# A state-space scan in one instruction over two PSUM banks instead of two instructions over one bank each

## What is computed

```python
deltaA = jnp.exp(jnp.einsum('bld,dn->bldn', delta, A))
deltaBu = jnp.einsum('bld,bln,bld->bldn', delta, B, u)
...
def step(h, inputs):
    dA_t, dBu_t, C_t = inputs
    h = h * dA_t + dBu_t
    y = jnp.einsum('bdn,bn->bd', h, C_t)
    return (h, y)
```

## Time and profile before

| | |
|---|---|
| median of 3 runs | 934.71 us (930.47 to 934.96) |
| profiled execution, its own time | 937.12 us |
| span of its trace, first to last instruction | 935.3 us |
| PE busy | 845.0 us (90%) |
| DVE busy | 633.1 us (68%) |
| ACT busy | 364.7 us (39%) |
| POOL busy | 349.3 us (37%) |
| mean granted TensorE clock | 0.955 of full speed |

### The profile page before, as it was taken

How to read it: one execution, slowest core, us unless ns; L and a number is a source line. 1 busy time by engine, 2 the same in 40 slices (tenths; PEclk the granted TensorE clock), 3 DMA queues, 4 the chain that set the end, 5 groups by cost and what they waited for, 6 DMA issues and landing times. The chain is left out here.

```text
span 935.3 us, 12349 instructions
## 1 busy us (share of the span) xinstructions
PE 845.0 (90%) x4548; PEld 632.7 (68%) x4548; DVE 633.1 (68%) x1218; ACT 364.7 (39%) x739; POOL 349.3 (37%) x337
## 2 busy tenths in 40 slices
PE   6898986788998999998999999997796999999996
PEld 5676754667536778876537878875134787738885
DVE  5342478998946278998944479996999877526222
ACT  5120345763273254443272354444384322261110
POOL 5300426851303047861312139840457521202221
PEclk9898997999998999999999999998789799999999
DMA  6202041023020244440020154321200123313542
GB/s 230 107 6 82 1 160 43 1 80 106 2 113 1 82 159 136 136 134 15 2 112 1 34 159 136 113 93 46 91 1 1 35 68 109 129 35 116 165 140 74
DMA packets 26927, 76.10 MB, mean 81 GB/s; under 512 B 3436, under 2 KB 5420, under 8 KB 26228
## 3 DMA queue, kind: packets, MB, share of 16 engines
q1 hardware_dynamic: 26612, 75.26, 24.2%
q10 hardware_dynamic: 256, 0.07, 0.0%
HBM read 74.13 MB, written 1.11 MB: 80 GB/s over the span
## 5 line engine op out<-in xcount | busy, mean ns | idle before, releaser
L915 PE MATMUL B<-late 128*128 128x256 f32 (+2 forms) x1064 | 243.1, 382 | 2.0 <-POOL late L698 1.1
L915 PEld LDWEIGHTS B<-late 128*128 128x128 f32 (+1 forms) x1064 | 199.4, 193 | 32.7 <-POOL late L698 2.0
L1599 DVE TENSOR_TENSOR_SCAN arena<-F,arena 128x512 f32<-128x512 f32 x128 | 149.1, 1206 | 3.3 <-POOL arena L590 2.4
L599 POOL TENSOR_TENSOR arena<-du,arena 128x1024 f32<-128x1024 f32 x60 | 140.9, 2358 | 23.1 <-PE F L915 23.1
L842 ACT ACTIVATE F<-delta,a_neg 128x255 f32<-128x255 f32 x256 | 109.3, 467 | 54.0 <-DVE arena L1599 53.7
L698 POOL TENSOR_TENSOR late<-late 128x512 f32<-128x512 f32 x42 | 53.5, 1275 | 137.4 <-DVE late L1744 101.7
L1609 DVE TENSOR_TENSOR arena<-arena,F 128x1024 f32<-128x1024 f32 x60 | 73.3, 1221 | 8.4 <-PE F L915 2.7
L579 POOL TENSOR_TENSOR rs<-ve,minus_half 128x2 f32<-128x2 f32 (+1 forms) x20 | 15.3, 764 | 165.6 <-DVE ve L1549 75.1
L904 ACT ACTIVATE late<-B 128x512 f32<-128x512 f32 x42 | 24.9, 593 | 93.7 <-PE B L915 93.6
L883 ACT ACTIVATE late<-B 128x512 f32<-128x512 f32 x96 | 51.9, 593 | 18.7 <-PE B L915 17.0
L915 PE MATMUL F<-arena,ident 128*128 128x256 f32 x232 | 57.9, 391 | 0.5 <-DVE arena L1637 0.5
(11 more groups left out here) (357 smaller groups left out, 1466.0 us busy)
## 6 DMA issues: line engine op xcount, KB each, us to landing
late<-in_w_moe SPq DMA_DIRECT2D x112, 384.0 KB, 3.5
room<-in_w_f SPq DMA_DIRECT2D x4, 2544.0 KB, 9.1
arena<-b_out SPq DMA_DIRECT2D x32, 256.0 KB, 5.5
room<-in_w_l SPq DMA_DIRECT2D x4, 768.0 KB, 6.4
w_m<-in_w_m SPq DMA_DIRECT2D x1, 2112.0 KB
room<-in_w_l SPq DMA_DIRECT2D x4, 512.0 KB, 3.7
x_t<-in_x_t SPq DMA_DIRECT2D x4, 256.0 KB, 2.6
x_tok<-in_x_tok SPq DMA_DIRECT2D x4, 256.0 KB, 5.3
```

Source lines behind the costliest of these rows:

```text
L599: g.tensor_tensor(state(n).rearrange("p d (s t) -> p d s t", s=2), du[:, 2 * dp:2 * dp + 2, :].unsqueeze(2).to_broadcast([P, 2, 2, S]), b_ ...
L915: return t_.matmul(dst, lhsT, rhs, start=start, stop=stop, skip_group_check=True)
L1599: v.tensor_tensor_scan(h, F[i][:, :], h, 0.0, ALU.mult, ALU.add)\
```

## The change

The two scans of a step become one instruction that reads the two neighbouring banks F[0] and F[1] as 1024 columns and writes both halves of the state. It waits for the second half of the refill (ACT works in order, so the first is then written too), and in step 0 for POOL's second input. It raises one semaphore step, `scan{n}`, where there were two, and both halves of the next refill wait for that one.

```diff
                 for i in range(2):
                     if n >= 1:
-                        act.wait_ge(*df.at(f"scan{n - 1}_{i}", b))
+                        act.wait_ge(*df.at(f"scan{n - 1}", b))
...
                     n = STEPS.index(ph)
-                    for i in range(2):
-                        h = state(n)[:, i, :]
-                        dve.wait_ge(*af.at(f"dA{n}_{i}", b))
-                        if n == 0:
-                            dve.wait_ge(*df.at("first", b))
-                            dve.wait_ge(*gf.at(f"dbu0_{i}", b))
-                        elif i == 0:
-                            dve.wait_ge(*gf.at(f"dbu{n}", b))
-                        v.tensor_tensor_scan(h, F[i][:, :], h, 0.0, ALU.mult, ALU.add)\
-                            .then_inc(df.step(f"scan{n}_{i}"), 1)
+                    dve.wait_ge(*af.at(f"dA{n}_1", b))
+                    if n == 0:
+                        dve.wait_ge(*df.at("first", b))
+                    dve.wait_ge(*gf.at(f"dbu{n}" if n else "dbu0_1", b))
+                    flat = state(n).rearrange("p i n -> p (i n)")
+                    v.tensor_tensor_scan(flat, banks_f[:, 0:1024], flat, 0.0, ALU.mult, ALU.add)\
+                        .then_inc(df.step(f"scan{n}"), 1)
```

## The result

The changed kernel takes **946.75 us**, the median of 4 runs (944.94 to 948.47). The kernel before took 932.59 beside it (4 runs, 929.38 to 934.96). The ratio is 1.017, with a 95% interval from 1.0141 to 1.0199: 14.2 us slower, where 12.3 were forecast. In the larger samples taken beside the experiments, the kernel before stands at 930.4 (12 runs), 930.3 and 930.1 (23 each). The changed kernel was not timed beside these; set against them, it would cost some 16 us.

What follows compares the result with a forecast made beforehand. DVE was taken to set the pace in stages 0 and 3 and run abreast with PE in 1 and 2. Stage terms 6.4, 2.9, 1.1 and 1.9 sum to 12.3 us; on 934.7, forecast 947.0 us, +1.3%, range 939 to 955.

Steps and rivals of the forecast that it cites:

- The bound: All four stages: DVE sets the pace in 0 and 3, abreast with PE in 1 and 2; PE loses behind DVE.
- rival A: PE has more slack than granted in stages 1 and 2; only 0 and 3 count, 943 or 941 us; chance 0.22.
- The scan itself: Each step's scan on DVE: one wide scan takes 2.27 us instead of 2.33, gaining 0.06 a step, 3.9 at most.
- The rule of one large tile that pays once: All 64 scans: whole fixed part of 0.14 us saved each, 926 us; the faster rival holding this had chance 0.03.
- DVE's busy time: Sign in the changed kernel's profile: DVE's busy time sinks by some 4 us.
- The plain step: Steps with only L1609 between scans: 0.50 us idle less 0.06 for the scan, +0.44, steps 4.01 apart.
- The step with table loads: Stage 0, loads on ACT behind the refill: +1.09 us less cover; steps 3, 5, 9 and 13 together 3.0.
- Tanh behind the refill: Stage 1 experts, L1738 waits for a tanh behind the refill: +0.73 us each at steps 7, 10 and 11.
- Step 0: Stage 0's first scan waits for the whole refill: +0.80 us.
- Stage by stage: Loss summed along the trace's steps: 6.4, 2.9, 1.1 and 1.9 us for stages 0 to 3, 12.3 in all.
- Stage 3: Up to step 9 +1.5 us, steps 13 to 15 +0.7, of which PE's slack takes 0.3: 1.9.
- Rival C: Worse: wide scan takes 2.41 us (7 us more), or the granted clock sinks (3 us); 950 to 957, chance 0.13.

Runs made afterwards that it cites:

- e5: Changed kernel with the wide scan only in sequences 1 and 2, two narrow scans in 0 and 3; 937.62 us, +7.3 against the kernel before.
- e10: Changed kernel with Tanh in place of Silu in sequence 1's feed-forward, so no table loads between stage 0's refills; 944.39 us.
- e12: Kernel before with Tanh in place of Silu in sequence 1's feed-forward, so no table loads there; 929.91 us, ratio 1.0001.
- e11: Changed kernel with four tanh of stage 1 moved on ACT ahead of the refill beside them; 944.67 us.
- e4: Changed kernel with each refill cut from four activations to three from step 1 on; 933.38 us, ratio 1.0036.
- e6: Changed kernel with the wide scan only in sequences 0 and 3, two narrow scans in 1 and 2; 945.26 us, ratio 1.0149.
- e8: Changed kernel, wide scan kept, with every refill after step 0 of a stage left out; 928.26 us, ratio 0.9970.
- e3: Kernel before, two scans kept, but both refill halves wait for the second scan and both scans for the whole refill; 948.76 us, +18.3.
- e1: Kernel before, two scans kept, but both halves of the refill wait for the second scan; 939.21 us, +8.8.

## Why the prediction was right, and where not

**The bound.** DVE was read as setting the pace in stages 0 and 3, and as running abreast with PE in 1 and 2, so that idle time on DVE would be passed on. The stage lengths bear it out in all four; e5 shows it for the middle ones alone, the place where rival A had its chance.

**The scan itself.** Forecast 2.27 us, measured 2.286 (mean of 64, had 1206 ns for 512 columns). The saving is 2.33 - 2.286 = 0.045 us a step instead of 0.06, 2.9 us in all. The rule of one large tile that pays once (the Trainium skill, "VectorE: DVE Perf Modes", "The TRN2 errata") would have given 926 us by the prediction's estimate: the rows disagree, since two neighbouring scans overlap and most of the fixed part was hidden already. DVE's busy time fell by 0.9 us, not by the 4 that were named. The scans gave 2.8; but a scan that starts 0.09 us before the end of L1609 (165.59 against 164.46 + 1.22 = 165.68) counts the common part once. In the trace before, 59 of the 64 steps begin so; in the trace after, 33. The other 26 no longer share some 0.085 us each, 2.2 us together.

**The plain step.** +0.44, 4.01 apart; measured 4.02 with an idle time of 0.41. The idle time ahead of all scans was put at some 20 us and is 15.1. **The step with table loads.** +1.09 at step 5; measured 4.68 - 3.58 = 1.10. e10 and e12 confirm that the cost is there only behind the wide scan. Their sum in stage 0 was put at 3.0 for four steps, plain part included, and came to 3.0 (0.78, 1.10, 0.77 and 0.36); e10 gets 2.5 of it back, since it leaves the plain part where it is.

**Tanh behind the refill.** The timeline of DVE in stage 1, step 7, of the changed kernel:

```profile
383.48 1.22 DVE L1606 TENSOR_TENSOR arena<-arena,F 128x1024 f32<-128x1024 f32 x1
385.62 0.69 DVE L1735 SCALAR_TENSOR_TENSOR late<-late,B 128x512 f32<-128x512 f32 x1 [0.93 <-ACT late L904]
386.41 0.69 DVE L1741 TENSOR_TENSOR late<-late,B 128x512 f32<-128x512 f32 x1
387.02 2.28 DVE L1596 TENSOR_TENSOR_SCAN arena<-F,arena 128x1024 f32<-128x1024 f32 x1
```

From L1606 to the scan 3.54 us, where it was 381.78 - 379.03 = 2.75: +0.79, less 0.045 for the scan, against 0.73 forecast. Here two products lie between the scans, and the scan itself doesn't wait; a wait by what stands behind the refill on ACT costs as much as one by the scan. e11 removes just that.

**Step 0.** Refill to scan:

```profile
142.06 2.29 DVE L1596 TENSOR_TENSOR_SCAN arena<-F,arena 128x1024 f32<-128x1024 f32 x1 [3.60 <-ACT F L842]
```

The refill started at 140.36; 1.70 us, against 143.22 - 142.32 = 0.90: +0.80, as forecast.

**Stage by stage.** Forecast 6.4, 2.9, 1.1, 1.9; measured 5.9 (with step 0), 3.0, 1.0, 4.0. Stage 0 is short of the forecast by 0.5 because of small instructions between steps 0 and 1: the scans of these steps are 10.59 apart where they were 11.33. L1414 took 0.17 instead of 1.98 us there, and L1502 2.17 instead of 1.05. The change does touch them, by way of POOL. The timelines of POOL and DVE, before:

```profile
143.15 9.26 POOL L599 TENSOR_TENSOR arena<-du,arena 128x1024 f32<-128x1024 f32 x4
150.46 1.98 DVE L1414 COPY tr<-v 128x4 f32<-128x4 f32 x1
```

and after:

```profile
140.76 9.26 POOL L599 TENSOR_TENSOR arena<-du,arena 128x1024 f32<-128x1024 f32 x4
150.37 0.17 DVE L1414 COPY tr<-v 128x4 f32<-128x4 f32 x1
```

Before, L1414 starts while POOL is in the last of its four multiplications and ends at 152.44, 0.03 us behind it (143.15 + 9.26 = 152.41). After, the last one has ended (150.02) when L1414 starts. L1502 and L1504 also end 0.03 us behind the end of one of POOL's four, in both. In all 14 traces L1414 takes 1.98 us where it starts before the last of the four has ended, and 0.17 where it starts behind it. So these instructions end by POOL's time, and what the first scan loses ahead of them is in part or whole made up: counted from the start of POOL's four, the scan of step 1 starts at 11.40 before and at 11.89 after, though the first scan starts at 0.07 and 1.30. In e4, e6 and e8 the first scan is wide too, but the refill ahead of it began earlier beside POOL's work: there it starts at 0.86 to 0.87 and the scan of step 1 at 11.37 to 11.39, so that nothing is left of step 0's loss. The prediction had no term for this; without it stage 0 would have cost some 6.7.

**Stage 3 is the step that failed**: "Up to step 9 +1.5, which the 6.66 us wait of PE passes on; steps 13 to 15 add 0.7", 1.9 in all. It was 4.0. ACT's timeline:

```profile
704.44 1.67 ACT L842 ACTIVATE F<-delta,a_neg 128x255 f32<-128x255 f32 x4 [1.36 <-DVE arena L1596]
706.05 2.14 ACT L883 ACTIVATE late<-B 128x512 f32<-128x512 f32 x4
```

PE's timeline, the instructions behind it:

```profile
707.16 0.39 PE L915 MATMUL B<-late,k_t 128*128 128x512 bf16 x1 [2.27 <-ACT late L883]
708.49 0.61 PE L915 MATMUL F<-bcp,pick 128*128 128x256 bf16 x2
708.89 1.91 PE L915 MATMUL F<-arena,ident 128*128 128x256 f32 x4
```

and DVE's:

```profile
706.14 2.29 DVE L1596 TENSOR_TENSOR_SCAN arena<-F,arena 128x1024 f32<-128x1024 f32 x1 [0.41 <-ACT F L842]
...
709.14 1.22 DVE L1606 TENSOR_TENSOR arena<-arena,F 128x1024 f32<-128x1024 f32 x1 [0.71 <-PE F L915]
```

The attention's exps (L883) stand behind the late refill, as the tanh does in stage 1. I had costed that for tanh, and for the exps only by a lump. PE waits 2.27 us for the first of them. The same wait in PE's timeline of the kernel before is 0.79:

```profile
697.21 0.88 PE L915 MATMUL B<-late,k_t 128*128 128x512 bf16 x2 [0.79 <-ACT late L883]
...
698.82 1.03 PE L915 MATMUL F<-arena,ident 128*128 128x256 f32 x4
```

In the changed kernel the granted clock is at its lower level, 1.2 GHz, behind this wait (columns of the earlier trace rows):

```profile
708.00:710.00 2.00, 2.00 (x13) 1.27 (x6) 1.29 (x2) 1.73 (x5) 0.00 (x0) 0.50 0.00 0
```

At the same distance from the scan of step 5 (which starts at 706.14, and at 696.98 before), it is 1.00 in the kernel before:

```profile
698.84:700.84 2.00, 1.44 (x8) 0.75 (x6) 1.90 (x3) 2.00 (x6) 0.85 (x1) 1.00 0.00 0
```

The four matmuls at 708.89 take 1.91 instead of 1.03 us, and DVE's L1606 waits for PE: 0.71 here, then 0.37, 0.65 and 0.49 in the next three steps, though the clock is back at 1.00 from 712 us on. From the scan of step 5 to that of step 9, the stage is 1.6 us longer than before (17.58 against 15.97).

Two causes are mixed in these 1.6 us, and the trace of e10 separates them. In stage 3, e10 has the code of the changed kernel. PE's timeline there:

```profile
703.66 0.39 PE L915 MATMUL B<-late,k_t 128*128 128x512 bf16 x1 [2.27 <-ACT late L883]
...
704.78 1.03 PE L915 MATMUL F<-arena,ident 128*128 128x256 f32 x4
```

The wait is the same 2.27 us, but the granted clock stays at 1.00 and the matmuls take 1.03. The same four steps take 16.87 us in e10, 0.9 longer than before, and L1606 waits for PE twice in them (0.27 and 0.81 us). So, by one trace of each, about 0.9 us of the 1.6 come from the late exps alone, and about 0.7 from the low clock. The low stretch is, at this place, in the traces of e3, e6 and e11 too, where stage 3 takes 80.2 to 80.4 us, and in none of the others. e1 also has late exps at the full clock, and these four steps are 1.3 us longer there. Why the clock fell behind this wait in one trace and not in the other stays open. e10's stage 3 is 79.92 all the same: every trace has a low stretch at the start of this stage, in e10 it lies some 2 to 3 us later, and one of the steps there takes 5.45 us where the changed kernel has 4.70. That the one makes the other is likely, not shown.

The rest of the miss is plainer. From the first scan to that of step 9 the stage is 3.4 us longer, where 1.5 was forecast: 1.8 of it up to the scan of step 5 (0.79 between the first two scans, 0.45 in the plain step before the scan of step 5), and the 1.6 above. The next three steps give 0.2 back, and the last three add 0.8, where 0.7 less 0.3 of slack was forecast. Rival C had the clock's part of this ("PE idles more in stages 0 and 3", some 3 us); it came on top of the forecast, at one place and with some 0.7 us.

**What offset it.** The forecast of 947.0 was made on a median of 934.7, from 3 runs; 12 and 23 runs put the kernel before at 930. The changed kernel is 16 us above that and not 12. So the time came out closer (946.75) than its terms did, and that is luck: the start was some 4 us too high, and the missing term of stage 3 was 2.1. The remaining 2 or so are of the size of the surplus outside the stages, which stays open.

**The page that warned.** "PSUM — Partial Sum Buffer" of the Trainium skill, specifications, has ScalarE and VectorE at full bandwidth in parallel on different banks. The trace agrees as far as it goes: in the kernel before, ACT writes one bank in 0.87 us while DVE reads the other at its usual 1.206. e3 shows that this use is lost by waits alone.

## What to carry to other kernels

Two instructions over two banks are a double buffer, and merging them takes it away: count what the producer must now do between the consumer's end and its next start (here 0.04 + 1.67 + 0.03 us against 1.24 us of other work) before counting the fixed cost saved, which neighbouring instructions may hide already (0.045 us here). A release of the whole and an acquire of the whole are each cheap alone and dear together, so look at both waits when one is made coarser. And follow the producer's queue past the refill: table loads, tanh and exps behind it moved as well. The loads made up 2.5 us of the loss (e10), the tanh 2.3 (e11), and the exps at least 0.9, of 14.

## What the runs showed beside

The granted clock differs between executions of the same instructions. The gap between stages 0 and 1 has the same code in the kernel before, the changed one and e6. A window of it that starts 80 us behind the last scan of stage 0 has (columns of the earlier trace rows), before:

```profile
289.70:299.70 10.00, 7.22 (x31) 5.60 (x30) 7.69 (x41) 3.46 (x9) 5.82 (x18) 0.73 0.00 0
```

and in e6:

```profile
292.70:302.70 10.00, 7.21 (x40) 5.93 (x40) 8.03 (x42) 4.22 (x11) 5.79 (x18) 1.00 0.00 0
```

PE is busy for 7.2 us in both, but gets through 31 matmuls in the first and 40 in the second. The changed kernel's window is like the first (granted clock 0.71, 30 matmuls). The gap is 136.0 us in the kernel before and in the changed one, and 133.1 in e6. Over all traces the head runs from 138.4 to 144.2 us and the gaps from 323.7 to 330.0, with no pattern that follows the edits, while an unchanged stage 1 or 2 repeats to within 0.1 us in most of them. So the kernel before can take 937 us in one execution (its profiled one) and 930 in the middle of 23, and three runs of it gave a median 4 us too high. For differences of a few us, lengths of stages in the trace were the sharper measure, and they say what the medians can't: where.

The other difference of this kind, L1414's 1.98 or 0.17 us at the same place, follows POOL's multiplications, as shown above under "Stage by stage".
